# Another written-out order of work for an attention block and its feed-forward part

## The reference

```python
y = x * rsqrt(mean(x * x, -1) + 1e-6) * rms_w            # RMS norm
q, k, v = split(y @ w_in.T)                              # 32 query heads, 8 groups of k and v, 64 wide
q, k = rope(q), rope(k)
attn = softmax(where(causal, q @ k.T * 64**-0.5, -inf))  # 1024 x 1024 for each of 2 x 32 heads
x = layernorm(x + (x + (attn @ v) @ w_out.T))
x_q = where(x > 0.33, 0.5, where(x < -0.33, -0.5, 0))    # ternary x
w   = where(weight > 0.2, 0.6, where(weight < -0.2, -0.6, 0)) + rram_variation
out = layernorm(x + x_q @ w.T)
```

## Time and profile before

| what | value |
|---|---|
| median of 3 runs | 1411.08 us (1410.71 to 1412.4) |
| the profiled execution's own time | 1412.32 us |
| its span, first to last instruction | 1410.5 us |
| mean granted PE clock | 0.983 of full |
| FIRST, up to the first prob_hi | 48.4 us |
| opening pass | 184.2 us |
| six middle passes | 158.7 to 159.7 us each |
| last pass with its tail | 222.6 us |

### The profile page before, as it was taken

How to read it: one execution, slowest core, us unless ns; L and a number is a source line. 1 busy time by engine, 2 the same in 40 slices (tenths; PEclk the granted TensorE clock), 3 DMA queues, 4 the chain that set the end, 5 groups by cost and what they waited for, 6 DMA issues and landing times. The chain is left out here.

```text
span 1410.5 us, 25319 instructions
## 1 busy us (share of the span) xinstructions
PE 1290.8 (92%) x7328; PEld 757.5 (54%) x7328; DVE 1182.6 (84%) x3062; ACT 1107.7 (79%) x2327; POOL 849.9 (60%) x904
## 2 busy tenths in 40 slices
...
GB/s 201 27 20 44 59 31 32 29 55 46 39 20 47 59 27 31 29 56 46 38 21 46 59 29 31 24 61 45 37 22 42 59 33 50 50 44 25 19 32 86
DMA packets 45163, 61.82 MB, mean 44 GB/s; under 512 B 10464, under 2 KB 27104, under 8 KB 45024
## 3 DMA queue, kind: packets, MB, share of 16 engines
...
## 5 line engine op out<-in xcount | busy, mean ns | idle before, releaser
L799 ACT ACTIVATE prob_hi<-t 128x512 f16<-128x512 f32 x576 | 340.2, 591 | 142.9 <-PE t L1225 137.8
L1104 DVE SCALAR_TENSOR_TENSOR prob_lo<-t,prob_hi 128x512 f16<-128x512 f32 x576 | 394.5, 686 | 58.8 <-ACT prob_hi L799 52.9
L831 ACT ACTIVATE prob<-prob,neg_max 128x896 f32<-128x896 f32 (+7 forms) x512 | 391.9, 767 | 8.9 <-DVE neg_max L1011 7.0
L1169 PE MATMUL s<-k_t,q_t 128*128 128x512 f16 (+3 forms) x1536 | 350.2, 330 | 32.3 <-DVE neg_max L1011 11.9
L1225 PE MATMUL t<-ident,prob 128*128 128x128 f32 x2304 | 351.5, 276 | 6.8 <-ACT prob L831 6.7
L1011 DVE CUSTOM_DVE_ANT_0 prob<-s,mask,neg_kappa 128x512 f32<-128x512 f32 (+3 forms) x512 | 320.0, 644 | 42.2 <-PE s L1169 24.8
L1225 PEld LDWEIGHTS t<-ident,prob 128*128 128x128 f32 x2304 | 290.5, 142 | 106.5 <-ACT prob L831 13.7
L1140 PE MATMUL ot<-prob_lo,v_sb 128*128 128x512 f16 x576 | 221.5, 385 | 29.8 <-DVE prob_lo L1104 28.9
L1138 PE MATMUL ot<-prob_hi,v_sb 128*128 128x512 f16 x576 | 220.4, 383 | 1.3 <-DVE o_raw L1085 1.0
L772 POOL TENSOR_TENSOR o_lo<-o_raw,o_hi 128x256 f16<-128x256 f32 x128 | 86.1, 672 | 196.3 <-ACT o_hi L907 194.7
L1169 PEld LDWEIGHTS s<-k_t,q_t 128*128 128x128 f16 x1536 | 137.5, 99 | 122.7 <-DVE neg_max L1011 37.2
(11 more groups left out here) (105 smaller groups left out, 1815.9 us busy)
## 6 DMA issues: line engine op xcount, KB each, us to landing
...
spread<-recip_rows SPq DMA_DIRECT2D x128, 128.0 KB
recip_rows<-turned SPq DMA_DIRECT2D x512, 0.5 KB
...
```

The costliest lines, as they stand in the source:

```text
L799: act.activation(prob_hi[:, u % 2, :], t_ps[u % 2][:, :], ACT.Copy, scale=P_SCALE).then_inc(prob_hi_done, 1)
L831: act.activation(row, row, ACT.Exp, bias=neg_max[:, kk % 4, h:h + 1], scale=-1.0, accum_out=total[:, kk % 4, h:h + 1]).then_inc(ex_done, 1)
L1104: dve.scalar_tensor_tensor(out=prob_lo[:, u % 2, :], in0=t_ps[u % 2][:, :], scalar=P_SCALE, in1=prob_hi[:, u % 2, :], op0=ALU.mult, op1=AL ...
L1169: mm = pe.matmul(s_ps[:, off:off + cols], q_t[:, h, s * P:(s + 1) * P], k_t[:, part, keys:keys + cols], start=(part == 0), stop=(part == 1))
```

## The change

Only the four tables of places are new: FIRST, OPENING, MIDDLE (used six times) and FINAL. Every operation, buffer, semaphore and wait rule stays, as does the rule that turns places into queues. In the old tables the exponentials of a tile stand in order of the head; in the new ones they may stand in any order. The diff, cut: FIRST and MIDDLE are whole; of OPENING and FINAL the lines that are spoken of below.

```diff
 
 
 FIRST = (
-    ('xn', 0), ('consts',), ('sq', 0), ('nq',), ('xn', 1), ('sw', 2, 0, 2), ('nw',), ('xn', 2), ('norm', 0),
-    ('w', 0), ('xn', 3), ('norm', 1), ('w', 1), ('norm', 2), ('norm', 3), ('w', 2), ('w', 3), ('sq', 1),
-    ('pj', 2, 0, 2), ('xn', 4), ('xn', 5), ('xn', 6), ('norm', 4), ('xn', 7), ('ro', 2, 0, 2), ('pj', 2, 0, 0),
-    ('norm', 5), ('vt', 2, 0), ('hl', 2, 0, 2), ('pj', 2, 0, 1), ('ro', 2, 0, 0), ('norm', 6), ('ro', 2, 0, 1),
-    ('hl', 2, 0, 0), ('hl', 2, 0, 1), ('sc', 2, 0, 0, 0), ('sc', 2, 0, 1, 0), ('norm', 7), ('sw', 2, 0, 0),
-    ('sw', 2, 0, 1), ('sc', 2, 0, 2, 0), ('sc', 2, 0, 3, 0), ('sc', 2, 1, 0, 0), ('sc', 2, 1, 1, 0),
-    ('ex', 2, 0, 0), ('ex', 2, 0, 1), ('ex', 2, 0, 2), ('ex', 2, 0, 3), ('ex', 2, 1, 0), ('sc', 2, 1, 2, 0),
-    ('ex', 2, 1, 1), ('ex', 2, 1, 2), ('sc', 2, 1, 3, 0), ('rc', 2, 0), ('rs', 2, 0), ('rc', 2, 1),
-    ('ex', 2, 1, 3), ('rs', 2, 1))
+    ('sq', 0), ('xn', 0), ('nq',), ('consts',), ('sw', 2, 0, 2), ('xn', 1), ('nw',), ('xn', 2), ('sw', 2, 0, 0),
+    ('norm', 0), ('norm', 1), ('xn', 3), ('w', 0), ('w', 1), ('norm', 2), ('w', 2), ('norm', 3), ('w', 3),
+    ('xn', 4), ('sq', 1), ('pj', 2, 0, 2), ('xn', 5), ('xn', 6), ('norm', 4), ('sw', 2, 0, 1), ('pj', 2, 0, 0),
+    ('ro', 2, 0, 2), ('norm', 5), ('xn', 7), ('hl', 2, 0, 2), ('pj', 2, 0, 1), ('vt', 2, 0), ('ro', 2, 0, 0),
+    ('norm', 6), ('ro', 2, 0, 1), ('norm', 7), ('hl', 2, 0, 0), ('hl', 2, 0, 1), ('sc', 2, 0, 0, 0),
+    ('sc', 2, 0, 1, 0), ('sc', 2, 0, 2, 0), ('sc', 2, 0, 3, 0), ('sc', 2, 1, 0, 0), ('ex', 2, 0, 2),
+    ('sc', 2, 1, 1, 0), ('ex', 2, 0, 1), ('sc', 2, 1, 2, 0), ('ex', 2, 0, 3), ('ex', 2, 0, 0), ('ex', 2, 1, 1),
+    ('ex', 2, 1, 0), ('ex', 2, 1, 2), ('sc', 2, 1, 3, 0), ('rc', 2, 0), ('rc', 2, 1), ('rs', 2, 0), ('rs', 2, 1),
+    ('ex', 2, 1, 3))
 
 OPENING = dict(
-    SCORES=(((0, 5, 8, 14), (10, 15, 15, 22), 46, 83), ((16, 21, 35, 38), (22, 32, 43, 47), 63, 91),
...
-    SQUARES=(0, 3),
-    NORMS=((8, 22), (22, 36), (37, 40), (42, 45), (46, 57), (66, 93), (99, 127), (151, 166)),
-    NORM_O=(18, 21),
-    W_OUT=(31, 61),
...
-    OUTPUT=((121, 213, 101, 263), (7, 11, 41, 70), (28, 48, 59, 63), (38, 49, 59, 71), (30, 32, 59, 93), (31, 54, 73, 94),
-         (47, 49, 66, 94), (23, 32, 50, 68), (15, 5, 19, 26), (17, 22, 24, 46), (12, 15, 41, 63), (22, 38, 47, 63),
-         (15, 48, 72, 90), (36, 56, 59, 72), (36, 48, 69, 94), (21, 35, 38, 65), (231, 119, 124, -31)))
+    SCORES=(((4, 8, 9, 9), (6, 22, 11, 6), 31, 54), ((22, 25, 34, 42), (44, 42, 43, 45), 48, 69),
...
+    SQUARES=(5, 32),
+    NORMS=((18, 23), (25, 35), (38, 42), (43, 45), (48, 78), (78, 103), (108, 134), (137, 167)),
+    NORM_O=(0, 4),
+    W_OUT=(20, 24),
...
+    OUTPUT=((121, 213, 101, 263), (18, 11, 32, 55), (37, 36, 69, 96), (45, 61, 73, 90), (53, 46, 63, 92),
+     (36, 48, 70, 97), (47, 26, 64, 110), (44, 52, 58, 81), (15, 24, 28, 40), (22, 30, 39, 48), (22, 34, 41, 61),
+     (46, 35, 55, 86), (44, 46, 58, 73), (26, 38, 57, 87), (37, 65, 65, 93), (23, 44, 46, 70), (231, 119, 124, -31)))
...
 MIDDLE = dict(
-    SCORES=(((0, 2, 2, 2), (3, 4, 6, 8), 24, 79), ((6, 7, 10, 24), (23, 29, 32, 36), 43, 114),
-         ((41, 41, 48, 50, 54, 54, 64, 70), (57, 58, 70, 73), 117, 169),
-         ((72, 75, 76, 81, 87, 89, 96, 100), (85, 85, 106, 119), 121, 217),
-         ((108, 113, 121, 132, 138, 150, 150, 157), (133, 153, 157, 160), 198, 222),
-         ((160, 163, 168, 173, 180, 191, 193, 209), (202, 204, 208, 214), 222, 286),
-         ((214, 219, 226, 233), (225, 230, 230, 245), 244, 304), ((234, 240, 240, 250), (253, 256, 257, 279), 288, 325),
-         ((252, 263, 273, 273), (285, 299, 301, 302), 331, 344), ((284, 284, 297, 300), (323, 328, 334, 335), 350, 359),
-         ((328, 328, 331, 334, 335, 336, 349, 351), (335, 348, 355, 360), 383, 384),
-         ((360, 366, 377, 377, 386, 387, 392, 393), (384, 386, 394, 405), 417, 423),
-         ((401, 402, 408, 414, 417, 428, 431, 442), (410, 424, 441, 451), 471, 487),
-         ((444, 454, 458, 458, 465, 465, 474, 484), (462, 476, 492, 495), 503, 516),
-         ((507, 513, 516, 520), (516, 523, 527, 532), 563, 573),
-         ((538, 545, 553, 562), (548, 549, 564, 566), 568, 574)),
-    PROJECT=((((53, 86, 99, 146), (119, 136, 153, 175), (155, 183, 194, 207)), 151),
-         (((206, 188, 222, 236), (214, 243, 262, 288), (251, 247, 280, 316)), 239),
-         (((311, 314, 331, 382), (330, 326, 346, 419), (389, 421, 438, 457)), 379),
-         (((433, 456, 455, 481), (477, 496, 503, 555), (498, 498, 541, 570)), 475)),
-    NORM_O=(25, 36),
-    W_OUT=(42, 55),
-    LOAD=204,
-    NORM_W=(238, 248),
-    W_IN=(252, 263, 285, 295),
-    OUTPUT=((15, 12, 27, 45), (14, 26, 37, 70), (36, 54, 56, 69), (38, 38, 67, 92), (39, 41, 72, 93), (38, 47, 76, 114),
-         (31, 69, 86, 100), (34, 47, 54, 82), (17, 21, 27, 39), (22, 25, 34, 45), (24, 20, 34, 62), (23, 23, 43, 75),
-         (22, 23, 48, 65), (22, 26, 30, 52), (21, 41, 51, 84), (12, -1, 32, 61), (-128, 233, 117, 110)))
+    SCORES=(((0, 0, 0, 0), (4, 5, 12, 12), 33, 54), ((9, 13, 23, 24), (35, 30, 26, 44), 42, 93),
+     ((35, 41, 41, 49, 50, 54, 58, 68), (70, 51, 68, 77), 106, 111),
+     ((73, 75, 78, 85, 90, 97, 97, 104), (89, 104, 96, 105), 142, 181),
+     ((105, 116, 120, 133, 141, 146, 149, 150), (144, 141, 157, 161), 189, 239),
+     ((161, 165, 167, 180, 181, 192, 197, 207), (183, 192, 206, 219), 224, 284),
+     ((207, 221, 225, 227), (238, 223, 235, 249), 285, 301), ((232, 237, 240, 248), (278, 260, 270, 263), 300, 314),
+     ((252, 266, 269, 276), (294, 290, 290, 286), 309, 336), ((281, 288, 295, 302), (321, 330, 312, 317), 354, 377),
+     ((317, 322, 330, 330, 334, 334, 344, 350), (330, 332, 365, 354), 386, 386),
+     ((356, 365, 373, 373, 385, 385, 389, 389), (383, 385, 405, 406), 438, 489),
+     ((400, 401, 407, 412, 421, 426, 436, 437), (422, 423, 444, 454), 485, 490),
+     ((447, 451, 454, 456, 468, 468, 486, 486), (477, 481, 492, 490), 501, 502),
+     ((506, 515, 517, 522), (528, 520, 528, 531), 552, 554), ((538, 545, 551, 559), (560, 564, 557, 561), 568, 575)),
+    PROJECT=((((53, 98, 77, 132), (112, 99, 136, 166), (146, 119, 156, 182)), 103),
+     (((192, 223, 187, 231), (219, 223, 252, 285), (254, 260, 279, 309)), 234),
+     (((299, 306, 350, 370), (329, 322, 388, 417), (388, 394, 448, 471)), 375),
+     (((436, 416, 452, 485), (482, 482, 518, 547), (499, 511, 546, 575)), 496)),
+    NORM_O=(19, 32),
+    W_OUT=(50, 54),
+    LOAD=220,
+    NORM_W=(233, 240),
+    W_IN=(253, 253, 278, 279),
+    OUTPUT=((15, 9, 27, 40), (24, 24, 36, 68), (26, 47, 59, 71), (39, 63, 69, 95), (47, 52, 60, 94),
+     (39, 38, 58, 124), (49, 46, 78, 96), (27, 46, 54, 71), (13, 16, 23, 36), (15, 18, 25, 45), (20, 17, 31, 63),
+     (39, 23, 48, 73), (29, 32, 52, 67), (16, 18, 35, 53), (25, 38, 54, 85), (14, 16, 38, 62), (-128, 233, 117, 110)))
...
 FINAL = dict(
-    SCORES=(((0, 3, 11, 12), (9, 9, 11, 16), 29, 60), ((20, 22, 25, 32), (27, 28, 35, 38), 53, 67),
-         ((37, 41, 43, 47, 49, 58, 60, 69), (54, 64, 71, 76), 84, 124),
...
-    NORM_O=(2, 14),
-    W_OUT=(23, 32),
-    FFN_IN=((26, 63), (51, 119), (147, 190), (229, 270)),
-    OUTPUT=((13, 8, 20, 29), (15, 13, 26, 46), (23, 26, 26, 60), (30, 54, 60, 70), (30, 52, 52, 64), (21, 20, 60, 86),
-         (22, 21, 62, 72), (12, 35, 52, 84), (12, 18, 33, 53), (16, 27, 50, 69), (37, 42, 62, 76), (48, 52, 62, 92),
-         (52, 52, 75, 108), (36, 77, 85, 98), (49, 43, 55, 94), (34, 29, 35, 63), (18, 26, 34, 67)),
-    LAYER=((317, 389, 407, 414, 419, 419, 449), (359, 392, 414, 431, 437, 444, 469), (388, 420, 437, 445, 450, 454, 474),
...
+    SCORES=(((0, 0, 0, 13), (12, 13, 5, 17), 20, 77), ((13, 22, 25, 32), (39, 37, 39, 40), 108, 115),
+     ((32, 43, 44, 48, 49, 51, 56, 58), (42, 62, 73, 64), 153, 166),
...
+    NORM_O=(0, 15),
+    W_OUT=(30, 35),
+    FFN_IN=((47, 76), (81, 133), (148, 212), (227, 265)),
+    OUTPUT=((12, 8, 25, 35), (23, 28, 34, 46), (19, 31, 36, 44), (22, 17, 43, 101), (47, 44, 74, 105),
+     (46, 40, 70, 96), (38, 30, 60, 77), (21, 33, 43, 81), (12, 6, 24, 46), (20, 28, 43, 58), (29, 44, 48, 60),
+     (37, 24, 56, 77), (36, 48, 64, 97), (53, 53, 74, 100), (43, 59, 60, 84), (13, 23, 32, 76), (23, 38, 47, 76)),
+    LAYER=((332, 373, 395, 407, 429, 432, 458), (349, 385, 415, 424, 442, 443, 470),
...
```

14 lines of the change are left out of this document (8 added, 6 removed), and 59 rows, old and new, of tables (LAYER, PROJECT, SCORES).

## The result

The changed kernel takes 1458.9 us (median of 4 runs, 1456.2 to 1462.7) against 1411.7 (4 runs beside them): ratio 1.033, 95% interval 1.030 to 1.036. It is slower by 3.3%; the forecast was 1400. Its profiled execution took 1459.0 us. Lines of the new kernel stand two lower than before (L1223 is the old L1225).

A forecast was written before the change was run, and what follows sets the result against it. PE, busy 92% of the span, bounds the kernel, with about 12 us waiting per middle pass. 1412.3 - 1.5 - 4 - 2.4 - 3 = 1401.4 profiled, 1400 for the median; range 1381 to 1420 leaves 2 in 10 out.

The forecast's parts named there:

- Middle, slots 60 to 66: End of each middle pass: late spread of tile (1, 5) makes op 1 5 wait 2.0 us; +2.1, ends 0 and +4.5.
- the forecast's own sum: Middle, slots 60 to 66: a 13.9 us chain to op 1 5 against 11.9 us of PE work, so 2.0 us waiting.
- Rival 1: New waits dominate in slots 66 and 39, slow matmuls follow: slots 60 to 66 cost 4.5, total 1415 or 1425; chance 0.22.
- Slots 0 to 4: Start of each middle pass: earlier prob_lo cuts PE's waits; -1.8 us, ends -3 and 0.
- the three moves that the text named: Middle pass start: two of six score steps leave slot 0, and oe 0 0 goes from slot 1 to 3.
- Slots 31 to 42: Middle pass: weight split leaves DVE's busiest stretch, -1.4, against op 0 7 waiting some 1.5; sum -0.4, ends -2 and +3.
- FIRST: Before the passes: turned v part and third x tile come earlier, each about 0.8; -1.5 us, ends -3 and +1.
- Opening: Opening pass: squares split over slots 0 and 4, op 0 7 two slots later; -4 us, ends -12 and +4.
- both named waits: Opening pass: DVE's 4.11 us at o_raw and op 0 7's 2.48 us, which the change was to relieve.
- the places that I had counted against it: Opening pass: four places where an sw now holds up a spread as in slot 60.
- Last: Last pass: prob_lo wait removed, -4 to -5, o_lo wait only moves to about 4 us; -3, ends -10 and +8.
- The tail has the same work.: Last pass: no gain or loss counted for its tail.

The follow-up runs named there:

- Run 3: Kernel before with one number changed: in middle passes the spread of tile (1, 5) issued in slot 62 instead of 52; 1470.3 us, ratio 1.042.
- run 4: Changed kernel with the middle passes' spread of tile (1, 5) issued in slot 57, ahead of the swap of projection (2, 1, 0), instead of 61; 1435.4 us, ratio 1.017.
- run 5: Changed kernel with two middle-pass spreads moved: tile (1, 5) to slot 57, tile (1, 7) to slot 64 behind the swap of (2, 1, 1); 1414.0 us, ratio 1.001.
- Run 7: Changed kernel, late spread kept; middle-pass oh 1 5 in slot 65, oe and on of tile (1, 6) a slot later, ro 2 1 0 behind; 1452.6 us, ratio 1.028.
- run 9: Kernel before with the new FINAL and the new places of all middle-pass events of slots 0 to 12 except projections; 1388.6 us, ratio 0.982.
- run 8: Kernel before with four middle-pass numbers changed: three score steps of tile (0, 3) to slot 1, oe 0 0 to slot 3; 1421.6 us, ratio 1.006.
- run 13: On top of run 5, the middle passes' spread of tile (0, 7) in slot 34 ahead of weight split w 3; 1417.0 us, ratio 1.005.
- run 14: On top of run 13, weight split w 3 late in slot 36 instead of 34, and projection (2, 0, 2) in slot 38 instead of 37; 1408.8 us, ratio 0.999.
- run 11: On top of run 5, the middle passes' swap of (1, 1, 2) issued ahead of its rotary part; 1411.1 us, ratio 0.998.

## Why the prediction was wrong

**The step that failed** is "Middle, slots 60 to 66": "So op 1 5 waits 2.0 us, and DVE stands at oe 1 6 meanwhile." The cause was right, the late spread behind sw 2 1 0 and its projection. The first to wait was wrong. I followed the tile's own chain to its end on TensorE in slot 66 and gave it all the work of slots 62 to 65 as cover. But a link of that chain, ScalarE's o_hi, sits in slot 62 of a strict queue with prob_hi of the next units behind it, and TensorE needs those in slot 64. Two sizes added to it. The chain from the projection's start to the end of o_lo took 15.7 us (713.05 to 728.79), not 13.9 (and the parts that I listed add up to 13.5 to 13.7): 5.6 us for the spread, with a second one issued 0.8 us behind it, where I had 4.3 to 4.5; the rest at hand-overs. And after 5.08 us of idling the matmuls of slots 64 to 66 ran at 0.61 to 0.63 us, the 1.2 GHz level, which the forecast left to a rival. Instead of +2.1 the place cost 7.6 more than before. Run 3 makes it from the old kernel with one number, runs 4 and 5 undo it.

Run 7 sorts the three errors, as an estimate. There op 1 5 is the first to wait, 3.6 us on average, near the 15.7 - 11.9 = 3.8 of the forecast's own sum with the true chain; the place costs 5.7. So the chain's length is worth some 1.5 of the 5.5 us that I missed, the slow matmuls some 2, and the first to wait some 2. The first error alone wouldn't have made the forecast wrong by this much.

**The same stretch held a second fault that I did not see:** in the new table rs 1 7 stands ahead of sw 2 1 1 on SyncE. The stall of slot 64 covered it; run 4 uncovered it, run 5 removed it (165.4 to 161.1 us per pass).

**Rival 1** had the stretch, the slow matmuls and the turning point ("used more than about 5 us after its issue"; it was 5.6), with 4.5 us where 7.6 came, again since it took op 1 5 as the one that waits.

**Slots 0 to 4:** -1.8 forecast, -2.0 measured up to slot 12 in the changed kernel; run 9 wins 1.6 per pass by it. DVE's o_raw no longer waits for o_lo, TensorE's waits there are 1.2 us in the lines above. Right, but only as a set: run 8 took the three moves that the text named, with one more, and lost 1.3.

**Slots 31 to 42:** -0.4 forecast. In slots 13 to 45 TensorE's waiting grew by 4.5 us per pass, the second large miss. op 0 7 waits 1.54 as forecast (1.5), and run 13, where that wait goes, bears out the reason given. Wrong was "the weight split leaves the busiest DVE stretch, which I put at -1.4": the waits for prob_lo in slots 34 and 37 did go, 1.8 us, but two splits back to back, 2.86 us, hold the mask step of slot 36 (1.4; run 14) and slot 33 waits 0.5 more. op 1 0, which I let start as before, waits 0.7 more in slot 41. Missed was vt 1 1, 1.91 us (GpSimd stands 5.25 us at a rotary part whose swap comes four slots later); run 11 shows that this order explains only 0.5 of it, the rest stays open.

**FIRST** -1.5 forecast, -0.6 measured, and that is scatter: the same new FIRST took 46.7 to 49.2 us in the eleven executions that have it and spreads in one copy, the old one 47.8 to 48.4 in five. **Opening** -4, measured +3.2 (+1.6 on the average of these executions): both named waits shrank (4.11 to 1.09, and 2.48 gone), but vt 0 1 now waits 3.72 us for GpSimd's rotary part and sc 0 4 0 2.33 for the lo part behind it; I had not followed that chain. op 1 1 waits 2.74, its spread issued just behind a swap, one of the places that I had counted against it. **Last** -3, measured -13.7, below my lower end. The 4.08 us wait went as forecast, op 0 1 waits 2.33, not 4. I set the end of the pass at nothing: "The tail has the same work." In the old order slot 64 had a wait of its own, and from slot 48 on the new order is 11.6 us shorter:

```profile
1355.46 0.90 PE L1225 MATMUL t<-ident,prob 128*128 128x128 f32 x3 [4.67 <-ACT prob L831]
```

The work was the same, the waits were not: I had not listed them there.

The sum of the terms with what was measured: 1412.3 - 0.6 + 3.2 + 58 - 13.7 = 1459.2, the profiled 1459.0. That the last pass won 10 us more than forecast was luck, and hid a part of the miss in the middle.
